# Row maxima of attention scores, taken over two neighbouring PSUM banks by one VectorE instruction

## The chip, the core and the metric

The program runs on one core of a Trainium2 chip. Its engines are TensorE (PE in the profile, its weight loads PEld), VectorE (DVE), ScalarE (ACT), GpSimd (POOL) and SyncE (SP), each with its own instruction queue; they meet only in semaphores and in the shared memories. PSUM, into which TensorE writes, has eight banks of 512 fp32 numbers for each of 128 partitions. The metric is the time on the device in microseconds, the median of several runs.

## The reference

Eight layers run over `x` of 8 sequences x 512 rows x 256 features, each added to its input: four pairs of an attention and a feed-forward part. The change touches the first three, called L0x, L0f and L1x, which share one function. L0x and L1x are plain cross attentions (kind "cross"), L0f is an attention over `x` itself with normalised queries, a temperature and a gate on its output (kind "mixture"). All three have 16 heads of 16 features:

```
q, k, v = heads(norm(x) @ Wq + bq), heads(ctx @ Wk + bk), heads(ctx @ Wv + bv)
attn = softmax(q @ k.T / sqrt(16))        # 512 x 512 for each head
x = x + merge(attn @ v) @ Wo + bo
# L0f: q = (q/|q| + query_embedding) * softplus(temperature); k, v from norm(x);
#      the output is scaled per row by gates from two softmaxes over the heads' output
```

The softmax subtracts each row's maximum before the exponential, and that maximum is what the change is about.

## The kernel before

`softmax_attentions` (L149) treats 24 items, three layers of 8 sequences. An item is one sequence in one layer. For each, q and k are split into bf16 parts, written to a scratch in memory and read back as `qstack` and `kstack`, so that one bf16 matmul with 96 rows gives a score of fp32 quality. Each item has 32 steps, numbered n = 0 to 31, with two units in each. Everything is written out by hand, and each engine runs its own list in the same order of steps:

- `for_maximum` (L753): a matmul with queries as rows, 128 x 512 into one bank of `ps_max`, 12 steps ahead (`LEAD`) of the scores. `maximum` (L482, reduction at L485) is VectorE's maximum over its 512 columns into `maxes`. After 16 units `negated` (L492, L494) writes minus the maxima as two bf16 parts, and TensorE turns them into the shared bank `ps_t` ("negmax", L827). ScalarE casts them into extra rows of `qstack` (L684, 1.86 us).
- `score` (L738, matmul L750): the transposed scores, 104 rows now with the maxima in them, into a bank of `ps_sc`. `exponentials` (L664, L671) is ScalarE's exp of it into `probs`.
- `values` (L774): at n = 1, 5, 9, ... a burst of 16 matmuls of `probs` with v into `ps_out`. ScalarE copies the sum to `heads_raw` (L679).
- Fills of the single bank `ps_t`: `TURNS` is a table of (step, what, which) that says in which step TensorE fills it with projections (k, q, v: L787, L795), transposes (xnT, hT, raw: L782, L833), negated maxima (L827) and output projections (y, L795), for the items one behind to two ahead. Before each fill TensorE waits until the former content was taken, by ScalarE or VectorE. VectorE takes raw by a reciprocal (L511) and a product into `htok` (L513), in its own list behind the maxima of the step before; for a mixture item it takes y into `ffo` (L594) with the scale that the gate arithmetic gives (L561 to L579, steps 20 and 21).

`ps_max` and `ps_sc` have three banks each, `ps_out` and `ps_t` one each, eight together. A matmul into a ring of three waits for the reduction or exponential three units before. The waits are, in `for_maximum` and `score`,

```
if at >= BANKS:
    pe.wait_ge(max_taken, at - BANKS + 1)      # probs_ready in score
```

Of the kernel before, what the change touches and what calls it, by code (L numbers as in the profile page):

```python
# [16 lines left out]
F32 = mybir.dt.float32  # L17
# [4 lines left out]
AX = mybir.AxisListType  # L22

P = 128
SEQS = 8
S = 512
# [78 lines left out]
STEPS = 32  # L105
# [43 lines left out]
def softmax_attentions(nc, T, G, name, kind):  # L149
# [9 lines left out]
    q_part, k_part = part_terms()  # L159
    ROWS = HD * len(q_part)  # L160
    LEAD = 12
    BANKS = 3
    SLOTS = 6
    PER = 4
    x_sb, ident, identb, own_rows = G["x"], G["ident"], G["identb"], G["own"]
    with Phase(nc, name) as ph:
# [21 lines left out]
        qstack = [ph.sb(f"qstack{b}", [ROWS + 8, HEADS, S], BF16) for b in range(2)]  # L188
        kstack = [ph.sb(f"kstack{b}", [ROWS + 8, HEADS, S], BF16) for b in range(2)]
        vpad = [ph.sb(f"vpad{b}", [P, TILES, HEADS * (HD + 1) + 15], F32) for b in range(2)]  # L190
        maxes = ph.sb("maxes", [P, TILES, HEADS], F32)
# [25 lines left out]
        gpart = ph.sb("gpart", [P, TILES], F32)  # L217
        ffo = ph.sb("ffo", [P, 2, D], F32)

        ps_max = ph.ps("ps_max", [P, BANKS, S], F32)  # L220
        ps_sc = ph.ps("ps_sc", [P, BANKS, S], F32)
        ps_out = ph.ps("ps_out", [P, S], F32)
        ps_t = ph.ps("ps_t", [P, S], F32)
# [10 lines left out]
        max_ps, max_taken, neg_step, negmax_ready = (ph.sem("max_ps"), ph.sem("max_taken"), ph.sem("neg_step"),  # L234
                                                     ph.sem("negmax_ready"))
# [21 lines left out]
        def due(q, n):  # L257

            if q.number == -2:
                return [(Item(0), w, c) for m, w, c in FIRST if m == n]  # L260
            near = [q.plus(k) for k in (-1, 0, 1, 2)]
            return [(x, w, c) for x in near if x.there for m, w, c in TURNS[x.kind]
                    if m == n and q.number + shift(w, c) == x.number and (x.later or w != "v")]
# [13 lines left out]
        def weights_here(engine, q):  # L277

            engine.wait_ge(weights_in[LAYERS[q.layer]], n_weights[q.kind])

        def own_key_rows(copy, stack):
            for g in range(4):
                for kt in range(TILES):
                    i = copy(stack[ROWS:ROWS + 8, 4 * g:4 * g + 4, kt * P:(kt + 1) * P], own_rows[ROWS:ROWS + 8])
            return i
# [151 lines left out]
        def _(dve):  # L437
            V = nc.vector
# [33 lines left out]
            def softplus_of_temperature():  # L472
                V.tensor_scalar(tmp1[:], temp[:], -1.0, None, ALU.mult).then_inc(sp_step, 1)
                dve.wait_ge(sp_step, 1)
                V.tensor_tensor(tmp2[:], tmp1[:], temp[:], ALU.min).then_inc(sp_step, 1)
                dve.wait_ge(sp_step, 4)
                V.scalar_tensor_tensor(out=softplus[:], in0=temp[:], scalar=0.0, in1=tmp3[:],
                                       op0=ALU.max, op1=ALU.add).then_inc(sp_step, 1)
                dve.wait_ge(sp_step, 5)
                V.tensor_tensor(qe_soft[:], qe[:], softplus[:], ALU.mult).then_inc(sp_step, 1)  # L480

            def maximum(q, unit):  # L482
                head, t = unit // 4, unit % 4
                dve.wait_ge(max_ps, q.count(64, unit + 1))
                V.tensor_reduce(maxes[:, t, head:head + 1], ps_max[:, q.count(64, unit) % BANKS, :], AX.X,  # L485
                                ALU.max).then_inc(max_taken, 1)

            def negated(q, g):

                own = maxes[:, :, 4 * g:4 * g + 4]  # L490
                dve.wait_ge(max_taken, q.count(64, 16 * g + 16))
                V.tensor_scalar(negmax[:, g % 2, :, :, 0], own, -1.0, None, ALU.mult).then_inc(neg_step, 1)  # L492
                dve.wait_ge(neg_step, q.count(4, g + 1))
                V.scalar_tensor_tensor(out=negmax[:, g % 2, :, :, 1], in0=own, scalar=-1.0,  # L494
                                       in1=negmax[:, g % 2, :, :, 0], op0=ALU.mult,
                                       op1=ALU.subtract).then_inc(negmax_ready, 1)

            def take_v(q, half):

                dve.wait_ge(in_bank["v"], q.count(2, half + 1))  # L500
                V.tensor_tensor(vpad[q.parity][:, 2 * half:2 * half + 2, 0:HEADS * (HD + 1)]
                                .rearrange("p b (h e) -> p b h e", h=HEADS)[:, :, :, 0:HD],
                                ps_t[:].rearrange("p (b h d) -> p b h d", b=2, h=HEADS),
                                weights[q.kind]["bv"][:].rearrange("p (h d) -> p h d", h=HEADS).unsqueeze(1)
                                .broadcast_to([P, 2, HEADS, HD]), ALU.add).then_inc(taken["v"], 1)
# [93 lines left out]
            def steps(q):  # L599
                prev, nxt, ahead = q.plus(-1), q.plus(1), q.plus(2)  # L600
                if nxt.there and nxt.later and nxt.seq == 0:
                    weights_here(dve, nxt)
                for n in range(STEPS):
                    for mine, w, c in due(q, n):
                        if w == "v":
                            take_v(mine, c)
                        if w == "q" and not mine.cross:
                            if c == 0 and mine.seq == 0:
                                weights_here(dve, mine)
                                softplus_of_temperature()  # L610
                            take_q(mine, c)
                        if w == "raw":
                            take_raw(mine, c)
                        if w == "gates":
                            gates_before_exp(mine)
                        if w == "y":
                            take_y(mine, c)
                    m = n + LEAD
                    own = q if m < STEPS else nxt
                    if own.there:  # L620
                        maximum(own, 2 * (m % STEPS))
                        maximum(own, 2 * (m % STEPS) + 1)
                        if m % 8 == 7:
                            negated(own, (m % STEPS) // 8)
                    if prev.there and not prev.cross and n == 20:
                        gates_after_exp(prev)
                    if prev.there and not prev.cross and n == 21:
                        gate_scale(prev)
                    if q.number == -1 and n == 16:

                        own_key_rows(V.tensor_copy, kstack[0]).then_inc(even_own_ready, 1)
                    if not ahead.there:
                        continue
                    if not ahead.cross and n == 12:
                        query_lengths(ahead)
                    if not ahead.later and n == FIRST_K_AT:
                        first_split(taken["k"], kf, kparts, k_step, k_split)
                    if not ahead.later and n == q_at["cross"]:
                        first_split(taken["q"], qf, qparts, q_step, q_split)
                    if ahead.later:  # L640
                        start = NORM_AT[ahead.kind]
                        if n in (start, start + 1):
                            statistics(ahead, (0, 1) if n == start else (2, 3))
                        if n == start + 2:
                            moments(ahead)
                        if n in (start + 4, start + 5):
                            normalised(ahead, (0, 1) if n == start + 4 else (2, 3))
# [5 lines left out]
        def _(act):  # L653
# [10 lines left out]
            def exponentials(q, n):  # L664
# [3 lines left out]
                for j in range(2):  # L668
                    at = q.count(64, 2 * n + j)
                    act.wait_ge(score_ps, at + 1)  # L670
                    nc.scalar.activation(probs[:, step % SLOTS, j], ps_sc[:, at % BANKS, :], ACT.Exp,  # L671
                                         scale=HD ** -0.5).then_inc(probs_ready, 1)
# [63 lines left out]
        def _(pe):  # L736
            weights_here(pe, Item(0))
            def score(q, n, j):  # L738
# [7 lines left out]
                at = q.count(64, 2 * n + j)  # L746
                if at >= BANKS:
                    pe.wait_ge(probs_ready, at - BANKS + 1)
                head = 4 * g + 2 * pair + j
# [3 lines left out]
            def for_maximum(q, unit):  # L753
                head, t = unit // 4, unit % 4
                if unit == 0:
                    pe.wait_ge(stack_in, q.count(192, 192))
                at = q.count(64, unit)
                if at >= BANKS:
                    pe.wait_ge(max_taken, at - BANKS + 1)
                nc.tensor.matmul(ps_max[:, at % BANKS, :], qstack[q.parity][0:ROWS, head, t * P:(t + 1) * P],  # L760
                                 kstack[q.parity][0:ROWS, head, :], start=True, stop=True).then_inc(max_ps, 1)

            def values(q, first, waited):
# [2209 lines left out]
def more_scratch(nc, T):  # L2973
# [4 lines left out]

PHASES = [
    (softmax_attentions, "L0x", ""),  # L2980
    (quantised_ffn, "L1f", ""),
    (feature_attention, "L2x", ""),
# [66 lines left out]
```

## Time and profile before

| what | us |
|---|---|
| median of 3 runs (4497.85 to 4503.6) | 4501.39 |
| the profiled execution | 4504.13 |
| its span | 4502.1 |
| TensorE busy, whole span | 4233.5 (94%) |
| VectorE busy | 2976.9 (66%) |
| ScalarE busy | 2544.5 (57%) |
| VectorE's maxima, L485, 1536 of them | 976.5, 683 ns each |
| ScalarE's exponentials, L671, 1536 of them | 822.7, 607 ns each |

The first 1750 us of the span are the three attentions; the feed-forward of L1 and the later layers follow. Scores start 68.20 us apart from one cross item to the next, and some 72 to 77 us apart in and around the mixture layer. Busy time of TensorE is modelled and overlaps between matmuls: a 512-column bf16 matmul shows 380 ns, but the next may start 0.22 us after it. So the starts of matmuls tell more than their durations. Idle time in square brackets names the instruction that ended it.

### The profile page before, as it was taken

Reading aid. Unit: us, or ns where it says so; the run is one execution under the profiler, and the core shown is the slowest. Engines: PE = TensorE matmul, PEld = TensorE weight load, DVE = VectorE, ACT = ScalarE, POOL = GpSimd, SP = SyncE. Lnnn points to the kernel's source line nnn. Section 1 sums busy time; section 2 is a strip of 40 time slices with the busy share of each in tenths; the row PEclk is TensorE's granted clock in tenths of the full one; section 3 lists DMA queues with packets and bytes.
Section 4 is the critical chain, followed back from the end, with each engine's and each line's share of the span. In section 5 each row is a group of like instructions: output and inputs, shape, how many; then the busy total and the mean of one; then the engine's idle time right before and its main releaser. Section 6 shows DMA issues by size and latency. Waiting matters only on the chain. (4 is left out here: it accounts for less than half of the span.)

```text
span 4502.1 us, 66443 instructions
## 1 busy us (share of the span) xinstructions
PE 4233.5 (94%) x23716; PEld 2403.0 (53%) x23750; DVE 2976.9 (66%) x7431; ACT 2544.5 (57%) x6408; POOL 810.4 (18%) x550
## 2 busy tenths in 40 slices
PE   6999999999999996778989999999999998999999
PEld 2344344444343343567545666666666665555555
DVE  5767777777767776867675666676776766344333
ACT  3767666666667765633555776767676775111111
POOL 2322444443322311523010000000000000000000
PEclk8999999999999998999999999999999999999999
DMA  8456455444456451000100110010101102000000
GB/s 161 73 76 87 65 63 85 54 69 63 74 75 84 69 71 61 1 15 15 75 12 27 31 32 28 30 36 26 33 27 32 32 27 73 5 5 5 10 5 10
DMA packets 182844, 204.97 MB, mean 46 GB/s; under 512 B 44651, under 2 KB 165099, under 8 KB 180854
## 3 DMA queue, kind: packets, MB, share of 16 engines
q1 hardware_dynamic: 180886, 199.15, 24.1%
q8 instruction: 192, 3.15, 0.3%
q10 hardware_dynamic: 1632, 1.57, 0.3%
q14 instruction: 134, 1.10, 0.1%
HBM read 139.90 MB, written 60.78 MB: 45 GB/s over the span
## 5 line engine op out<-in xcount | busy, mean ns | idle before, releaser
L485 DVE TENSOR_REDUCE L0x_maxes<-L0x_ps_max 128x1 f32<-128x512 f32 x1536 | 976.5, 683 | 291.0 <-PE L0x_ps_max L760 289.3
L671 ACT ACTIVATE L0x_probs<-L0x_ps_sc 128x512 f32<-128x512 f32 x1536 | 822.7, 607 | 362.3 <-PE L0x_ps_sc L750 358.3
L760 PE MATMUL L0x_ps_max<-L0x_kstack,L0x_qstack 96*128 96x512 bf16 x1536 | 588.0, 384 | 22.7 <-DVE L0x_maxes L485 21.3
L2756 ACT ACTIVATE L3x_pexp<-L3x_ps,L3x_nmax 128x77 f32<-128x77 f32 (+2 forms) x1536 | 601.4, 433 | 0.0
L750 PE MATMUL L0x_ps_sc<-L0x_qstack,L0x_kstack 104*128 104x512 bf16 x1536 | 557.7, 384 | 11.5 <-ACT L0x_probs L671 11.0
L2638 DVE TENSOR_REDUCE L3x_nmax<-L3x_ps 128x2 f32<-128x154 f32 (+2 forms) x768 | 346.3, 506 | 242.1 <-PE L3x_ps L2869 239.7
L2764 ACT COPY L3x_pT<-L3x_ps 128x512 f32<-128x512 f32 x512 | 275.1, 593 | 225.8 <-PE L3x_ps L2877 225.4
L2256 ACT ACTIVATE L3f_act_g<-L3f_ps_gu 128x512 f32<-128x512 f32 x128 | 76.4, 597 | 542.2 <-PE L3f_ps_gu L2302 542.1
L774 PE MATMUL L0x_ps_out<-L0x_probs,L0x_vpad 128*32 128x512 f32 x3072 | 371.0, 601 | 1.1 <-ACT L0x_probs L671 1.1
L2654 DVE TENSOR_SCALAR L3x_pexp<-L3x_pexp,L3x_rsum 128x77 f32<-128x77 f32 (+2 forms) x1536 | 357.7, 306 | 6.8
L2756 ACT ACTIVATION_READ_ACCUMULATOR L3x_pexp<-L3x_ps,L3x_nmax 128x1 f32 x1536 | 359.4, 235 | 0.0
L2199 DVE TENSOR_TENSOR L3f_h<-L3f_act_g,L3f_ps_gu 128x512 f32<-128x512 f32 x128 | 88.0, 687 | 383.1 <-ACT L3f_act_g L2256 382.9
L760 PEld LDWEIGHTS L0x_ps_max<-L0x_kstack,L0x_qstack 96*128 96x128 bf16 x1536 | 151.0, 98 | 282.5 <-DVE L0x_maxes L485 167.5
L2895 PE MATMUL L3x_ps<-L3x_pT,L3x_v 128*64 128x128 f32 x4096 | 279.9, 279 | 0.7 <-ACT L3x_oT L2772 0.7
L2877 PEld LDWEIGHTS L3x_ps<-ident,L3x_pexp 128*128 128x128 f32 x2048 | 239.1, 141 | 73.4 <-issue 55.5
L2877 PE MATMUL L3x_ps<-ident,L3x_pexp 128*128 128x128 f32 x2048 | 266.1, 273 | 0.9 <-DVE L3x_pexp L2654 0.9
L750 PEld LDWEIGHTS L0x_ps_sc<-L0x_qstack,L0x_kstack 104*128 104x128 bf16 x1536 | 150.6, 98 | 211.7 <-ACT L0x_probs L671 81.1
L2599 POOL TENSOR_TENSOR L3x_v<-L3x_v,L3x_relv 128x256 f32<-128x256 f32 x32 | 23.4, 731 | 1294.7 <-ACT L3x_v L2739 1294.7
L2302 PE MATMUL L3f_ps_gu<-L3f_xnT,L3f_wg 128*128 128x512 f32 x512 | 243.0, 597 | 2.1 <-DMA L3f_wd<-in_L3f_wd 2.1
L2313 PE MATMUL L3f_ps_y<-L3f_wd,L3f_h 128*128 128x256 f32 x1024 | 242.4, 380 | 1.5 <-DVE x_res L2209 1.5
L2895 PEld LDWEIGHTS L3x_ps<-L3x_pT,L3x_v 128*64 128x64 f32 x4096 | 218.3, 136 | 43.4 <-issue 42.5
L2302 PE MATMUL L3f_ps_gu<-L3f_xnT,L3f_wu 128*128 128x512 f32 x512 | 240.6, 592 | 0.0
(377 smaller groups left out, 6841.4 us busy)
## 6 DMA issues: line engine op xcount, KB each, us to landing
L0x_kstack<-parts_scratch SPq DMA_DIRECT2D x141, 256.0 KB, 10.0
L0x_qstack<-parts_scratch SPq DMA_DIRECT2D x141, 256.0 KB, 14.5
parts_scratch<-L0x_kparts SPq DMA_DIRECT2D x24, 768.0 KB, 3.7
parts_scratch<-L0x_qparts SPq DMA_DIRECT2D x24, 768.0 KB, 5.0
rel_scratch<-L3x_rel_e SPq DMA_DIRECT2D x32, 408.0 KB, 2.4
L3x_rel_d<-prob_scratch SPq DMA_DIRECT2D x32, 408.0 KB, 3.1
L0x_kv_in<-in_ctxT SPq DMA_DIRECT2D x16, 512.0 KB, 4.5
L3x_rel_t<-rel_scratch SPq DMA_DIRECT2D x32, 154.0 KB, 2.4
```

Source lines behind the costliest of these rows:

```text
L485: V.tensor_reduce(maxes[:, t, head:head + 1], ps_max[:, q.count(64, unit) % BANKS, :], AX.X, ALU.max).then_inc(max_taken, 1)
L671: nc.scalar.activation(probs[:, step % SLOTS, j], ps_sc[:, at % BANKS, :], ACT.Exp, scale=HD ** -0.5).then_inc(probs_ready, 1)
L750: nc.tensor.matmul(ps_sc[:, at % BANKS, :], kstack[q.parity][:, head, kt * P:(kt + 1) * P], qstack[q.parity][:, head, :], start=True, stop ...
L760: nc.tensor.matmul(ps_max[:, at % BANKS, :], qstack[q.parity][0:ROWS, head, t * P:(t + 1) * P], kstack[q.parity][0:ROWS, head, :], start=T ...
L774: i = nc.tensor.matmul(ps_out[32 * j:32 * j + 32, :], vpad[q.parity][:, kt, (HD + 1) * head:(HD + 1) * head + 32], probs[:, q.count(STEPS, ...
L2302: i = nc.tensor.matmul(ps_gu[:, n % 2, k], w[:, ci, n * P:(n + 1) * P], xnT[:, ci, :], start=(ci == 0), stop=(ci == C - 1))
L2638: i = V.tensor_reduce(nmax[:, n % 4, s], ps[:, bank:bank + 2, a:b], AX.X, ALU.max, negate=True)
L2654: i = V.tensor_scalar(pexp[:, m % 4, e, a:b], pexp[:, m % 4, e, a:b], rsum[:, m % 4, s, e:e + 1], None, ALU.mult)
L2756: i = nc.scalar.activation(pexp[:, n % 4, e, a:b], ps[:, SB + 2 * (n % 2) + e, a:b], ACT.Exp, bias=nmax[:, n % 4, s, e:e + 1], accum_out=s ...
L2764: nc.scalar.copy(pT[:, m % 2, e], ps[:, TB + e]).then_inc(pt_ready, 1)
L2877: i = nc.tensor.transpose(ps[:, TB + e, kt * P:(kt + 1) * P], pexp[:, m % 4, e, kt * P:(kt + 1) * P], ident[:])
L2895: i = nc.tensor.matmul(ps[DIMH * e:DIMH * (e + 1), OB, at:at + P], v[g % 2][:, vt, h * DIMH:(h + 1) * DIMH], pT[:, m % 2, e, kt * P:(kt + ...
```

## The change

The six banks are divided anew: four for maxima, as two neighbouring pairs, and two for scores. TensorE fills both banks of a pair with the two units of a step; VectorE waits for both and takes the maxima of 2 x 512 columns by one instruction. TensorE waits for the release of a pair only ahead of its first matmul. `maximum` becomes `maxima`, `max_taken` counts steps instead of units, and the counts that others wait for follow. Scores keep their code, with `BANKS` 2 in place of 3, so each waits for the exponential two units before. Nothing is computed differently.

```diff
-    BANKS = 3
+    PAIRS_OF_MAXIMA = 2
+    BANKS = 2
...
-        ps_max = ph.ps("ps_max", [P, BANKS, S], F32)
+        ps_max = ph.ps("ps_max", [P, PAIRS_OF_MAXIMA, 2, S], F32)
...
-            def maximum(q, unit):
-                head, t = unit // 4, unit % 4
-                dve.wait_ge(max_ps, q.count(64, unit + 1))
-                V.tensor_reduce(maxes[:, t, head:head + 1], ps_max[:, q.count(64, unit) % BANKS, :], AX.X,
+            def maxima(q, step):
+                head, t = step // 2, 2 * (step % 2)
+                at = q.count(STEPS, step)
+                dve.wait_ge(max_ps, 2 * at + 2)
+                V.tensor_reduce(maxes[:, t:t + 2, head], ps_max[:, at % PAIRS_OF_MAXIMA], AX.X,
                                 ALU.max).then_inc(max_taken, 1)
...
-                dve.wait_ge(max_taken, q.count(64, 16 * g + 16))
+                dve.wait_ge(max_taken, q.count(STEPS, 8 * g + 8))
...
-                        maximum(own, 2 * (m % STEPS))
-                        maximum(own, 2 * (m % STEPS) + 1)
+                        maxima(own, m % STEPS)
...
-                at = q.count(64, unit)
-                if at >= BANKS:
-                    pe.wait_ge(max_taken, at - BANKS + 1)
-                nc.tensor.matmul(ps_max[:, at % BANKS, :], qstack[q.parity][0:ROWS, head, t * P:(t + 1) * P],
+                at = q.count(STEPS, unit // 2)
+                if unit % 2 == 0 and at >= PAIRS_OF_MAXIMA:
+                    pe.wait_ge(max_taken, at - PAIRS_OF_MAXIMA + 1)
+                nc.tensor.matmul(ps_max[:, at % PAIRS_OF_MAXIMA, unit % 2], qstack[q.parity][0:ROWS, head, t * P:(t + 1) * P],
```

No matmul moves in TensorE's list, only its waits do. In the list before, from a burst of value matmuls through the fill with raw heads to the fill with negated maxima, every maximum matmul waits:

```order
L760 MATMUL L0x_ps_max<-L0x_kstack,L0x_qstack 128x512 [waits L0x_max_taken]
L750 MATMUL L0x_ps_sc<-L0x_qstack,L0x_kstack 128x512 [waits L0x_probs_ready]
L760 MATMUL L0x_ps_max<-L0x_kstack,L0x_qstack 128x512 [waits L0x_max_taken]
L833 MATMUL L0x_ps_t<-ident,L0x_heads_raw 128x128 [waits L0x_out_taken,L0x_raw_taken]
L833 MATMUL L0x_ps_t<-ident,L0x_heads_raw 128x128 x3
```

In the changed list at the same place (its lines are one or two further down) every second one does, and the scores' waits look the same but ask for one exponential more:

```order
L761 MATMUL L0x_ps_max<-L0x_kstack,L0x_qstack 128x512 [waits L0x_max_taken]
L751 MATMUL L0x_ps_sc<-L0x_qstack,L0x_kstack 128x512 [waits L0x_probs_ready]
L761 MATMUL L0x_ps_max<-L0x_kstack,L0x_qstack 128x512
L834 MATMUL L0x_ps_t<-ident,L0x_heads_raw 128x128 [waits L0x_out_taken,L0x_raw_taken]
L834 MATMUL L0x_ps_t<-ident,L0x_heads_raw 128x128 x3
```

On VectorE two neighbouring reductions become one in place; what stood behind the second stands behind the wide one.

## Rows read from the trace of the kernel before

**Rows 1.** Windows: us, busy us of PE, PEld, DVE, ACT, POOL, granted clock, DMA, GB/s

```profile
412.76:480.96 68.20, 66.16 (x354) 27.07 (x353) 48.99 (x98) 47.27 (x81) 19.71 (x12) 1.00 0.54 78
```

**Rows 2.** Waits of TensorE's weight loads, 75 to 1750 us: total, times, longest

```profile
PEld L0x_ps_max L760 <- DVE L0x_maxes L485: 158.6, 227, 2.8
...
PEld L0x_ps_sc L750 <- ACT L0x_probs L671: 81.1, 185, 0.9
```

**Rows 3.** VectorE's groups by shape: count, busy us, mean ns, idle before

```profile
L485 DVE TENSOR_REDUCE L0x_maxes<-L0x_ps_max 128x1 f32<-128x512 f32 x1536 | 976.5, 683 | 291.0 <-PE L0x_ps_max L760 289.3
L2638 DVE TENSOR_REDUCE L3x_nmax<-L3x_ps 128x2 f32<-128x838 f32 x256 | 261.1, 1020 | 0.0
...
L2638 DVE TENSOR_REDUCE L3x_nmax<-L3x_ps 128x2 f32<-128x154 f32 x256 | 81.5, 318 | 242.1 <-PE L3x_ps L2869 239.7
```

**Rows 4.** Timeline, steps 2 to 5: start us, us, what; PE, then DVE, then ACT

```profile
417.21 0.60 PE L750 MATMUL L0x_ps_sc<-L0x_qstack,L0x_kstack 104*128 104x512 bf16 x2
...
417.86 0.38 PE L750 MATMUL L0x_ps_sc<-L0x_qstack,L0x_kstack 104*128 104x512 bf16 x1
...
418.34 0.39 PE L750 MATMUL L0x_ps_sc<-L0x_qstack,L0x_kstack 104*128 104x512 bf16 x1
418.56 0.38 PE L760 MATMUL L0x_ps_max<-L0x_kstack,L0x_qstack 96*128 96x512 bf16 x1
...
421.05 0.39 PE L827 MATMUL L0x_ps_t<-identb,L0x_negmax 128*8 128x128 bf16 x4 [0.16 <-DVE L0x_htok L513]
...
417.41 2.54 DVE L485 TENSOR_REDUCE L0x_maxes<-L0x_ps_max 128x1 f32<-128x512 f32 x4 [0.87 <-PE L0x_ps_max L760]
...
420.57 0.42 DVE L513 TENSOR_TENSOR L0x_htok<-L0x_ps_t,L0x_rden 128x256 f32<-128x256 f32 x1
...
417.68 1.09 ACT L671 ACTIVATE L0x_probs<-L0x_ps_sc 128x512 f32<-128x512 f32 x2 [2.24 <-PE L0x_ps_sc L750]
```

**Rows 5.** Timeline, steps 26 to 29 of the item before

```profile
405.54 0.38 PE L760 MATMUL L0x_ps_max<-L0x_kstack,L0x_qstack 96*128 96x512 bf16 x1
...
407.42 0.38 PE L827 MATMUL L0x_ps_t<-identb,L0x_negmax 128*8 128x128 bf16 x4
...
404.30 2.54 DVE L485 TENSOR_REDUCE L0x_maxes<-L0x_ps_max 128x1 f32<-128x512 f32 x4 [2.94 <-PE L0x_ps_max L760]
...
404.67 1.08 ACT L671 ACTIVATE L0x_probs<-L0x_ps_sc 128x512 f32<-128x512 f32 x2
```

**Rows 6.** Timeline, steps 14 to 16 (374 us), 21 to 25 (393 to 400 us)

```profile
374.43 1.34 DVE L485 TENSOR_REDUCE L0x_maxes<-L0x_ps_max 128x1 f32<-128x512 f32 x2 [1.35 <-PE L0x_ps_max L760]
...
376.45 0.48 PE L795 MATMUL L0x_ps_t<-L0x_wo_cross,L0x_hT 128*128 128x256 f32 x1
...
399.67 0.39 PE L750 MATMUL L0x_ps_sc<-L0x_qstack,L0x_kstack 104*128 104x512 bf16 x1
...
393.63 3.17 ACT L671 ACTIVATE L0x_probs<-L0x_ps_sc 128x512 f32<-128x512 f32 x6
...
399.03 1.56 ACT L671 ACTIVATE L0x_probs<-L0x_ps_sc 128x512 f32<-128x512 f32 x3
```

**Rows 7.** Timeline, steps 30 to 1, across the start of an item at 412.76

```profile
414.21 0.39 PE L760 MATMUL L0x_ps_max<-L0x_kstack,L0x_qstack 96*128 96x512 bf16 x1
...
414.80 0.39 PE L760 MATMUL L0x_ps_max<-L0x_kstack,L0x_qstack 96*128 96x512 bf16 x1
...
412.87 2.47 DVE L485 TENSOR_REDUCE L0x_maxes<-L0x_ps_max 128x1 f32<-128x512 f32 x4
```

**Rows 8.** Mixture item, step 23: timeline of PE and DVE, then the window behind it

```profile
983.56 0.39 PE L760 MATMUL L0x_ps_max<-L0x_kstack,L0x_qstack 96*128 96x512 bf16 x1 [2.55 <-DVE L0x_maxes L485]
983.79 0.38 PE L795 MATMUL L0x_ps_t<-L0x_wo_mixture,L0x_hT 128*128 128x256 f32 x1
...
982.03 0.88 DVE L594 SCALAR_TENSOR_TENSOR L0x_ffo<-L0x_ps_t,L0x_gscale,L0x_bo_mixture 128x256 f32<-128x256 f32 x2
...
984.00:988.00 4.00, 4.00 (x13) 2.35 (x12) 2.71 (x6) 0.80 (x2) 3.92 (x3) 0.59 0.26 88
```

## The prediction

> **What bounds the kernel now.** The page's chain of waits covers only the last stage, the gated experts, so I read the stage that the change touches, the first 1750 us, from views of its own. First the windows: one sequence of a cross layer takes 68.20 us, and TensorE is busy for 66.16 of them, VectorE for 48.99 (72%), ScalarE for 47.27 (69%) [rows 1]. TensorE is the bound, and it works through one fixed order. What counts is therefore how long that order stands still, not how busy another engine is. Next the waits: weight loads of TensorE wait 158.6 us for the release of a bank of maxima [rows 2]. Most of that lies under matmuls still running, so it is a ceiling. The true loss is read from the starts of matmuls, which follow one another by 0.22 us when nothing holds them (418.34, 418.56) [rows 4]. Read in this way, a steady cross sequence loses about 1.3 us to maxima: 0.50 at steps 0 and 1, where the matmul of 414.21 is one of three held up [rows 7], and the rest at steps 8 and 13. In a mixture sequence one such wait alone is 2.55 us [rows 8].
>
> **The change, part by part.** Three things happen. (1) 1536 reductions of 512 become 768 of 1024. (2) The reduction starts when the second of its two matmuls is in, and frees both banks at its end. (3) Scores have two banks, so score i waits for exponential i-2, not i-3. TensorE's order of instructions stays.
>
> *Width.* Back to back, four reductions take 2.48 to 2.54 us, so a further one costs 0.60 [rows 4, 5], two 1.20. A wide one is not in this stage, but the same instruction form elsewhere reads PSUM: 154 elements in 318 ns, 838 in 1020, which is 1.03 ns an element and gives 1.21 us for 1024 [rows 3]. Bounds: 1.13 (1.21 less the overlap of 0.08 seen between neighbours) and 1.37 (two times the 683 ns of a narrow one). I take 1.21 to the end, 1.13 in a row. That saves 0.07 x 768 = 54 us of VectorE's work, none of it on the path by itself. The Trainium skill, "Perfetto Trace Analysis", section "Optimizing Scalar/DVE Operations", gives about 125 ns of fixed cost for an instruction on PSUM and says that grouping pays when the engine is saturated; by its figure the saving would be an estimated 96 us of work. The row of 72% says that the engine is not saturated. The same section says that where an unsaturated engine leaves bubbles on others, breaking instructions up may help, which is against this change.
>
> *What it does to the path.* I walked one steady cross sequence of 32 steps in bundles of four, each from one burst of value matmuls to the next, since the burst (1.86 us) lets both helpers catch up. Rules, from rows: a matmul's result starts ScalarE or VectorE 0.42 to 0.47 us after the matmul starts (417.21 to 417.68), exponentials follow by 0.49 and last 0.60, and the freed matmul starts 0.06 after their end (418.28 to 418.34) [rows 4].
>
> Steps 2 to 5, +0.74. Scores of step 3 now wait for the exponentials of step 2, ending 418.28 and 418.77: they start at 418.34 and 418.83 instead of 417.86 and 418.34. The second maximum matmul of step 3 goes from 418.56 to 419.06; the wide reduction starts at 419.48 and ends at 420.69, where four narrow ones ended at 419.95 [rows 4]. Behind it on VectorE are negation, reciprocal and the product into htok, and TensorE's fill of the shared bank ps_t at 421.05 waits for exactly that product. It comes 0.74 later.
>
> Steps 26 to 29, +0.82. The same: exponentials of step 26 from 404.67 to 405.75 put the second maximum matmul of step 27 from 405.54 to 406.03, its reduction ends at 407.66, not 406.84, and the fill with the negated maxima goes from 407.42 to 408.24 [rows 5].
>
> Steps 14 to 17 and 22 to 25, +0.53 each. Two reductions, 1.34 us from 374.43, end at 375.77; the wide one can start when the second narrow one did, since both wait for the second matmul (375.77 - 0.68 = 375.09), and ends at 376.30. The products behind it and the fill at 376.45 that waits for them come 0.53 later [rows 6]. One row stands for both places.
>
> Third score bank, bare, +0.84 more. At step 21 the second score waits 0.19 longer and at step 22 0.16 more, for exponentials that resume at 393.63 after a cast: +0.35. At step 25 the exponentials from 399.03 free the score of 399.67 only at 400.17: +0.49 [rows 6].
>
> Steps 30 to 1, +0.54. The product behind the wide reduction of step 30 is 0.76 late. The reduction of step 31 starts at 413.63 instead of 412.87 and ends at 414.84, so the matmul of 414.21 starts at 414.90; the last before the burst goes from 414.80 to 415.34 [rows 7]. The waits of 0.50 at steps 0 and 1, which the change is aimed at, are swallowed by this.
>
> Steps 6 to 9, +0.09 (the 0.49 wait for a maximum goes, scores lose 0.59); steps 10 to 13, -0.05 (0.17 gained, 0.12 lost behind the negation).
>
> Sum: 0.74 + 0.82 + 1.06 + 0.84 + 0.54 + 0.09 - 0.05 = 4.04 us on 68.20.
>
> *Mixture sequences*, walked in the same way, have the same bundles at steps 26 to 1 (+0.82, +0.54), +1.02 in steps 14 to 17 (0.53 behind the product, 0.49 for the score bank), and +0.20 and +0.23 in steps 2 to 5 and 10 to 13: +2.8. Against it, VectorE's long gate arithmetic makes TensorE wait 2.55 us for a maximum of step 23, to 983.56 [rows 8]. With four banks that matmul is free, but the next instruction, the second output fill, needs ffo, ready at 982.91 and 0.34 later by the wide reductions ahead of it: the fill goes from 983.79 to 983.3, 0.5 saved, and 1.9 us of standstill remain, that is 0.7 less. From 984 to 988 the granted clock is 0.59 [rows 8], which is mostly its lower level of 1.2 GHz, behind that standstill. In these 4 us TensorE starts 13 matmuls where 18 would fit at 0.22, so if the shorter standstill keeps the clock, some 1.2 us come back as well. I take that: 2.8 - 0.5 - 1.2, about +1.2 a sequence with rounding up; if not, +2.3.
>
> *Total.* Of 24 sequences some 12 are steady cross (12 x 4.04 = 48), 5 are full mixture with the gate wait (5 x 1.2 = 6), 7 lie between (7 x 3.2 = 22, taken between the two kinds): +76 us. The rest of the program is untouched. The profiled execution took 4504.1 for a span of 4502.1; the sum is made against it, and the median of the runs shown is 4501.4, so 4501.4 + 76 = 4577.
>
> **Rivals.** *Faster.* The 1.3 us of a cross sequence and 3.7 of a mixture one that maxima cost today disappear and nothing comes in their place: 12 x 1.3 + 7 x 1.8 + 5 x 3.7 = 47, or 4454. For it: VectorE is 0.07 faster a pair and leads by four banks. It decides if the fills of ps_t do not stand right behind the chain maxima, negation, product; the rows show them 0.06 behind (420.99 to 421.05). [...] *Only the VectorE half holds.* If scores lose nothing, the four fills still come 0.25, 0.53, 0.53 and 0.33 late, and 1.2 is saved: +0.4 x 24, or 4510. Against it: the third bank is used whenever a score starts before exponential i-2 has ended, as at 417.86 against 418.28. *The clock.* If the added stops bring the lower clock once in most sequences, as after 984, 1.2 us x 20 comes on top: 4601. Against it: each added stop is under 1 us, and the sequence at 412.76 to 480.96, with several such, has clock 1.00 [rows 1]. *Width.* At 1.37 us a reduction, four fills are 0.16 later: +0.6 x 24, 4592, inside my range.
>
> **How the numbers follow.** About 0.2% (9 us) can be told from no change. Forecast 0.72, faster rival 0.07, VectorE half alone 0.11 (it straddles the border: half of it counts as same, some as slower), clock 0.10. Range 4530 to 4608: below, half of what I let add up is absorbed by other waits; above, the clock or the width. Faster 0.07, same 0.06, slower 0.87.
>
> **What would show it.** In the profile after: a wide reduction of 1.21 us; a steady cross sequence of about 72.2 us; waits of TensorE for the exponentials (now 81.1 us ahead of weight loads [rows 2]) clearly up, those for maxima down, those for htok and negmax up by 0.5 to 0.8 a place; the clock at the gate stop of five sequences near 1. Wrong would be a period of 68 or less, or fills that no longer stand behind htok.

## The result and the profile after

The changed kernel takes 4589.19 us, the median of four runs (4588.57 to 4590.2); the kernel before took 4502.5 beside it. The ratio is 1.019, 95% interval 1.0177 to 1.0203: slower by 87 us. The profiled execution has a span of 4588.2 us against 4502.1.

The attentions carry all of it. Their last score starts at 1835.0 us in the trace after and at 1746.6 before, 88.4 later; what follows is 2.4 shorter. The 24 sequences are numbered 0 to 23 from here on: 0 to 7 are of L0x, 8 to 15 of the mixture layer, 16 to 23 of L1x. First a steady cross sequence, number 5, the same one as in [rows 1]; the columns are those of that group:

```profile
430.30:502.35 72.05, 66.87 (x353) 26.07 (x354) 47.31 (x66) 48.02 (x81) 19.68 (x12) 1.00 0.51 74
```

It takes 72.05 us, where it took 68.20. VectorE has less to do (47.31 for 48.99), TensorE keeps its full clock, and the time went up by 3.85. The waits of TensorE over the three layers, 75 to 1840 us (total, times, longest; first weight loads, then matmuls):

```profile
PEld L0x_ps_sc L751 <- ACT L0x_probs L672: 263.3, 611, 1.1
...
PEld L0x_ps_max L761 <- DVE L0x_maxes L487: 94.9, 137, 0.8
```

```profile
PE L0x_ps_sc L751 <- ACT L0x_probs L672: 39.8, 113, 0.6
PE L0x_ps_t L828 <- DVE L0x_negmax L496: 20.9, 40, 2.3
PE L0x_ps_t L828 <- DVE L0x_htok L515: 20.9, 23, 0.9
PE L0x_ps_t L788 <- DVE L0x_htok L515: 9.1, 16, 0.6
PE L0x_ps_t L796 <- DVE L0x_htok L515: 8.1, 16, 0.6
```

Against [rows 2], waits for maxima fell from 158.6 to 94.9 and waits for exponentials rose from 81.1 to 263.3. New names stand among the waits of the matmuls: fills of `ps_t` wait for `htok` and `negmax`. The wide reduction itself, in VectorE's groups by shape (75 to 1840 us, so 758 of the 768), takes 1221 ns, for two of 683 in [rows 3]:

```profile
L487 DVE TENSOR_REDUCE L0x_maxes<-L0x_ps_max 128x2 f32<-128x1024 f32 x758 | 919.3, 1221 | 417.4 <-PE L0x_ps_max L761 415.6
```

Steps 3 to 5 of the same sequence, which answer to [rows 4]:

```profile
435.80 0.39 PE L751 MATMUL L0x_ps_sc<-L0x_qstack,L0x_kstack 104*128 104x512 bf16 x1 [0.32 <-ACT L0x_probs L672]
...
436.29 0.39 PE L751 MATMUL L0x_ps_sc<-L0x_qstack,L0x_kstack 104*128 104x512 bf16 x1
...
436.52 0.38 PE L761 MATMUL L0x_ps_max<-L0x_kstack,L0x_qstack 96*128 96x512 bf16 x1
...
436.93 1.23 DVE L487 TENSOR_REDUCE L0x_maxes<-L0x_ps_max 128x2 f32<-128x1024 f32 x1 [0.18 <-PE L0x_ps_max L761]
...
438.19 0.18 DVE L494 TENSOR_SCALAR L0x_negmax<-L0x_maxes 128x16 bf16<-128x16 f32 x1
...
438.78 0.42 DVE L515 TENSOR_TENSOR L0x_htok<-L0x_ps_t,L0x_rden 128x256 f32<-128x256 f32 x1
...
439.26 0.39 PE L828 MATMUL L0x_ps_t<-identb,L0x_negmax 128*8 128x128 bf16 x4 [0.89 <-DVE L0x_htok L515]
```

This is the chain of the prediction, link by link: the scores 0.49 apart behind exponentials, the last maximum matmul at 436.52, the wide reduction 0.41 behind it, then negation, reciprocal and product, and the fill 0.06 after the product's end. The fill's idle time in brackets is 0.89 where [rows 4] has 0.16.

### The profile page after: what moved, and what is told of

It is laid out like the page before. It is cut to its first block and busy times, and to the rows that moved or that the text cites. A ratio compares the mean times of both kernels' runs of the same rounds, so it can differ in the third digit from the quotient of the medians.

```text
span 4588.2 us, 65675 instructions
## 1 busy us (share of the span) xinstructions
PE 4264.7 (93%) x23716; PEld 2376.5 (52%) x23750; DVE 2940.4 (64%) x6663; ACT 2561.3 (56%) x6408; POOL 808.7 (18%) x550
## 5 line engine op out<-in xcount | busy, mean ns | idle before, releaser
L487 DVE TENSOR_REDUCE L0x_maxes<-L0x_ps_max 128x2 f32<-128x1024 f32 x768 | 931.0, 1221 | 429.3 <-PE L0x_ps_max L761 427.5
L672 ACT ACTIVATE L0x_probs<-L0x_ps_sc 128x512 f32<-128x512 f32 x1536 | 841.6, 603 | 386.1 <-PE L0x_ps_sc L751 374.0
L751 PEld LDWEIGHTS L0x_ps_sc<-L0x_qstack,L0x_kstack 104*128 104x128 bf16 x1536 | 149.0, 97 | 373.6 <-ACT L0x_probs L672 263.3
L2878 PE MATMUL L3x_ps<-ident,L3x_pexp 128*128 128x128 f32 x2048 | 266.1, 273 | 0.9 <-DVE L3x_pexp L2655 0.9
```

The lines of the kernel that those rows point to most:

```text
L487: V.tensor_reduce(maxes[:, t:t + 2, head], ps_max[:, at % PAIRS_OF_MAXIMA], AX.X, ALU.max).then_inc(max_taken, 1)
L751: nc.tensor.matmul(ps_sc[:, at % BANKS, :], kstack[q.parity][:, head, kt * P:(kt + 1) * P], qstack[q.parity][:, head, :], start=True, stop ...
L2878: i = nc.tensor.transpose(ps[:, TB + e, kt * P:(kt + 1) * P], pexp[:, m % 4, e, kt * P:(kt + 1) * P], ident[:])
```

## The experiments

The table shows eight stretches of a steady cross sequence in four kernels, with the time that TensorE's starts lose in each: the distance of a start to the next, less what the same instruction takes when nothing holds it (0.22 us for a maximum or score). The two kernels in the middle are experiments and follow below. Stretches run from one burst of value matmuls to the next.

| steps | before | 4 + 2 banks, narrow | and started late | after | after - before | predicted |
|---|---|---|---|---|---|---|
| 2 to 5 | 1.09 | 1.41 | 1.89 | 1.83 | +0.74 | +0.74 |
| 6 to 9 | 0.66 | 0.75 | 0.76 | 0.76 | +0.09 | +0.09 |
| 10 to 13 | 1.38 | 1.19 | 1.46 | 1.33 | -0.05 | -0.05 |
| 14 to 17 | 0.66 | 0.63 | 1.25 | 1.18 | +0.52 | +0.53 |
| 18 to 21 | 0.49 | 0.67 | 0.67 | 0.68 | +0.19 | +0.19 |
| 22 to 25 | 0.48 | 1.11 | 1.71 | 1.65 | +1.17 | +1.18 |
| 26 to 29 | 1.09 | 1.49 | 1.98 | 1.91 | +0.82 | +0.82 |
| 30 to 1 | 0.51 | 0.55 | 0.56 | 0.82 | +0.32 | +0.54 |
| period | 68.2 | 69.7 | 72.2 | 72.05 | +3.85 | +4.04 |

The eight differences add up to 3.80; the other 0.05 us of the period is not in stops that this table counts.

**The banks alone.** Two kernels keep 1536 narrow reductions, each started by its own matmul. The first has three banks for maxima and two for scores, the second four and two. Their edit, with `MAX_BANKS` 3 or 4:

```diff
-    BANKS = 3
+    MAX_BANKS = 3
+    BANKS = 2
...
-                if at >= BANKS:
-                    pe.wait_ge(max_taken, at - BANKS + 1)
-                nc.tensor.matmul(ps_max[:, at % BANKS, :], qstack[q.parity][0:ROWS, head, t * P:(t + 1) * P],
+                if at >= MAX_BANKS:
+                    pe.wait_ge(max_taken, at - MAX_BANKS + 1)
+                nc.tensor.matmul(ps_max[:, at % MAX_BANKS, :], qstack[q.parity][0:ROWS, head, t * P:(t + 1) * P],
```

> The kernel before with two score banks in place of three; maxima stay narrow in three banks, one bank unused. Theory (two causes add up: the missing third score bank, and the later end of the wide reduction ahead of the ps_t fills): the missing bank alone costs about 1.9 us of a steady cross sequence (68.2 to 70.1), some 42 us in all, near 4545. Rival A (the score bank costs everything, the width nothing): about 4589, as the changed kernel. Rival B (the wide reduction costs everything): 4502.

> Four banks for maxima and two for scores as in the changed kernel, but one narrow reduction for each bank, so only the width differs from the changed kernel. Theory: waits for maxima fall below those of three banks, the score waits stay, a steady cross sequence takes about 69.9 us, total near 4535; the width is then the other 55 us. Rival A: 4589, as with the wide reduction. Rival B: 4502 or less.

Measured: 4543.18, ratio 1.0086 (1.0071 to 1.0101), and 4531.66, ratio 1.006 (1.0045 to 1.0075); a steady cross period is 69.9 and 69.7. Taking the third bank from the scores costs 38 us. In the first kernel it lies idle; giving it to the maxima, as the second does, buys back 12, mostly outside the steady sequences. Both times come within 4 us of what was expected. Not all of the 38 is waits for a bank: sequence 8 takes 5.3 us of it, and there a negation that otherwise lasts 0.18 us takes 2.15 beside a GpSimd instruction, of which the last experiment tells. The fourth bank does not pay for the third one that the scores lose.

**The late start alone.** The kernel before, with one number changed: the first reduction of a step waits for the second matmul too. Then the same on top of four banks for maxima and two for scores, which makes it the changed kernel in everything except the width.

```diff
-                dve.wait_ge(max_ps, q.count(64, unit + 1))
+                dve.wait_ge(max_ps, q.count(64, 2 * (unit // 2) + 2))
```

> The kernel before, three and three banks, with one wait stretched: the first of the two narrow reductions of a step also waits for the step's second matmul. Nothing else changes. Theory: the late start is what costs in the wide reduction, since the fills of ps_t stand behind it; the end of the second reduction comes 0.6 us later after each burst, about +2.4 us in a steady cross sequence plus some 0.5 at three banks, total near 4565. Rival A (only the score bank costs): within 5 us of 4502.

> Four banks for maxima, two for scores, narrow reductions, but the first reduction of a step waits for the step's second matmul, as the wide one must. Against the run with four narrow banks (4531.7) only that wait is added; against the changed kernel only the width differs, with the wide reduction 0.06 us shorter than the two narrow ones. Theory: the late start is the whole cost of the wide reduction, so this takes what the changed kernel takes or up to 0.06 us x 4 a sequence more, 4589 to 4597. Rival (something else in the wide instruction costs, such as its reading of two banks against TensorE's writes): near 4532 to 4545.

Measured: 4592.97, ratio 1.0195 (1.018 to 1.021), and 4579.92, ratio 1.0172 (1.0155 to 1.0189). Both miss, the first by 28 us, the second by 9 below its range. With three banks the late start was dearer than expected, as dear as the whole change: the period is 72.2, and the negations held in sequences 6 and 7 take 2.13 us. The ring of three is short for pairs: weight loads wait 266.1 us for maxima (158.6 before, [rows 2]):

```profile
PEld L0x_ps_max L760 <- DVE L0x_maxes L485: 266.1, 491, 3.1
```

With four banks the period is 72.19, within 0.14 of the changed kernel's. The steps 3 to 5 of this kernel, in sequence 5 again:

```profile
437.08 2.70 DVE L486 TENSOR_REDUCE L0x_maxes<-L0x_ps_max 128x1 f32<-128x512 f32 x4 [0.97 <-PE L0x_ps_max L761]
...
440.41 0.42 DVE L514 TENSOR_TENSOR L0x_htok<-L0x_ps_t,L0x_rden 128x256 f32<-128x256 f32 x1
...
440.89 0.33 PE L828 MATMUL L0x_ps_t<-identb,L0x_negmax 128*8 128x128 bf16 x3 [0.96 <-DVE L0x_htok L514]
```

In a steady sequence the change is then two prices and a rebate: 1.54 for the banks (68.19 to 69.73), 2.46 for the late start (69.73 to 72.19), and 0.14 back for the width. In the table the late start stands at five places, each with a fill of `ps_t` behind VectorE: 0.48, 0.27, 0.62, 0.60 and 0.49, together 2.46. The rebate is a net figure. Most stretches gain, 0.39 together, and steps 30 to 1 lose 0.26. There a maximum at step 1 waits 0.31 for the wide reduction, which frees its two banks only at its end; with narrow reductions, started just as late, no maximum waits there.

The whole program does not follow the steady sequences. The changed kernel takes 9.3 us more than the one with four banks and late narrow reductions, though each steady sequence takes 0.14 less. The difference lies mostly in sequences 6 to 8: 75.6, 72.9 and 73.0 us there, 80.3, 78.2 and 76.6 in the changed kernel. It is no price of the width as such, but of where VectorE's small instructions meet GpSimd's, which the last experiment takes up: once they are kept apart in sequences 6 to 8, the changed kernel takes 4575.71, 4.2 less than this one. The 48 us from 4531.66 to 4579.92 are not the late start alone either: sequence 8 gets 2.3 us shorter by it, 75.3 to 73.0, since the negation that was held there is no longer.

**The opposite split.** Two banks for maxima, four for scores, narrow reductions (`MAX_BANKS = 2`, `BANKS = 4` in the first diff).

> The kernel before with two banks for maxima, four for scores, narrow reductions: the opposite division. Theory (each ring pays with its own turnround: matmul to release takes 0.42 + 0.60 + 0.06 = 1.1 us at ScalarE, 0.42 + 0.68 + 0.06 = 1.2 at VectorE, so a ring of two stops TensorE wherever four score and maximum matmuls stand within 0.88 us, whichever ring it is): the maxima ring of two costs at least what the score ring of two cost (38 us), rather more since a reduction is longer: 4545 to 4560, a cross period of 70 to 70.7. Rival (only scores are short of banks, maxima have slack, and a fourth score bank takes away the waits of 0.5 us at steps 21 to 29): 4490 to 4500, faster than before.

Measured: 4567.7 (4558.56 to 4568.96), ratio 1.0139 (1.0122 to 1.0156). The cross period is 70.7, at the upper end of what was expected; the time lies 8 us above the range, and the full mixture sequences take 78.5 us (75.3 to 76.6 before). Its two windows, one cross and one mixture sequence, and its wait for maxima:

```profile
430.67:501.39 70.72, 67.85 (x354) 27.00 (x353) 49.10 (x98) 47.61 (x81) 19.68 (x12) 1.00 0.52 75
955.74:1034.25 78.51, 73.15 (x386) 32.93 (x385) 58.45 (x122) 47.91 (x82) 34.15 (x15) 0.96 0.45 61
```

```profile
PEld L0x_ps_max L761 <- DVE L0x_maxes L486: 338.4, 673, 3.5
```

A bank more for either ring is paid for by the other. Three and three is the best of the four splits that were run.

**Another step for the raw heads.** If the late chain maxima, negation, product is what counts, fills that do not wait for `htok` at once should give it room. The fill with raw heads goes two steps later or one earlier, so that the fill behind it is a step further away. The table is edited alike in the changed kernel and in the one before; the fence shows pieces of its lines.

```diff
-    "cross": [(4, "raw", 3), (5, "negmax", 1), (9,
+    "cross": [(5, "negmax", 1), (6, "raw", 3), (9,
...
-(14, "xnT", 0), (15, "raw", 0), (16, "y", 0)
+(14, "raw", 0), (15, "xnT", 0), (16, "y", 0)
...
-(23, "raw", 1), (24, "q", 0), (26, "q", 1), (29, "negmax", 0), (31, "raw", 2)
+(22, "raw", 1), (24, "q", 0), (26, "q", 1), (29, "negmax", 0), (30, "raw", 2)
```

(In the mixture table 4, 15, 25 and 31 become 6, 17, 26 and 30.)

> The changed kernel with the raw fills of ps_t moved so that each comes right behind a burst of value matmuls or has no fill in the step after it (cross: steps 4, 15, 23, 31 to 6, 14, 22, 30, with xnT 0 from 14 to 15; mixture: 4, 15, 25, 31 to 6, 17, 26, 30). VectorE then has taken raw before the next fill asks. Theory: the waits of fills for htok (0.79, 0.89 and 0.53 of 1.06 us in a cross sequence) go, about -2 us a sequence, near 4545. Rival (the fills wait for something else that ends at the same time, or the product moves and the wait with it): within 10 us of 4589.

> The kernel before with the raw fills moved as in the run on the changed kernel. There the waits for htok went, but scores, no longer kept apart by the raw fills, gave 1.3 of 2.3 us back with two banks. Theory (three banks of scores do what the fills did): here the waits for htok (0.32, 0.34, 0.36 us a sequence) and for the heads (0.64) go and little comes back, about -1.2 us a sequence, near 4478. Rival (the give-back is in ScalarE's pace whatever the banks): 4495 to 4505.

Measured: 4582.56, ratio 1.0171 (1.0154 to 1.0188), and 4518.81, ratio 1.0031 (1.0018 to 1.0044). Both miss their forecasts of 4545 and 4478, the second on the other side of no change. The chain did get its room: on the changed kernel the lost time at steps 5, 16 and 24 goes from 1.06, 0.80 and 0.89 to 0.53, 0.08 and 0. But the period falls only from 72.05 to 71.08. Steps 4 and 5 of sequence 5 show where the rest went:

```profile
433.38 0.39 PE L751 MATMUL L0x_ps_sc<-L0x_qstack,L0x_kstack 104*128 104x512 bf16 x1 [0.37 <-ACT L0x_probs L672]
...
434.85 0.22 PE L828 MATMUL L0x_ps_t<-identb,L0x_negmax 128*8 128x128 bf16 x1 [0.37 <-DVE L0x_negmax L496]
```

The raw fill at step 4 had also been the work that TensorE did while ScalarE caught up. Without it the scores of step 4 wait 0.54, where they had waited for nothing, and those of steps 23 and 31 0.48 each. In the kernel before the same happens with three banks (the raw fill's own wait of 0.64 at step 4 goes, a score's wait of 0.54 comes, and a maximum of step 8 waits 0.31 longer), its period goes from 68.2 to 68.3, and all but one of the mixture sequences become longer. What I had overlooked is that ScalarE falls behind TensorE at the same places as VectorE, and that a fill is cover for both.

**GpSimd's hold on VectorE.** In sequences 6 to 8, where the mixture layer begins, the change cost 6.7, 6.9 and 5.3 us instead of the 3.2 that I had put down. The first of them ends so in the trace after (GpSimd, VectorE, then TensorE, and the window behind it):

```profile
571.61 2.12 POOL L381 TENSOR_TENSOR L0x_qparts<-L0x_qf,L0x_qparts 128x1024 bf16<-128x1024 f32 x1
571.66 2.11 DVE L494 TENSOR_SCALAR L0x_negmax<-L0x_maxes 128x16 bf16<-128x16 f32 x1
...
573.80 0.18 DVE L496 SCALAR_TENSOR_TENSOR L0x_negmax<-L0x_maxes,L0x_negmax 128x16 bf16<-128x16 f32 x1
...
574.12 0.58 PE L828 MATMUL L0x_ps_t<-identb,L0x_negmax 128*8 128x128 bf16 x4 [2.29 <-DVE L0x_negmax L496]
...
575.04 0.63 PE L761 MATMUL L0x_ps_max<-L0x_kstack,L0x_qstack 96*128 96x512 bf16 x1
```

```profile
574.10:578.10 4.00, 3.98 (x16) 1.15 (x20) 2.23 (x2) 2.94 (x3) 0.00 (x0) 0.50 0.56 197
```

A negation of 16 numbers a partition, 0.18 us elsewhere, takes 2.11, starts 0.05 after an instruction of GpSimd and ends with it. TensorE waits 2.29 us for the negation and then works at a granted clock of 0.50, the lower of its two levels (1.2 GHz). Before, the negation fell into the second half of the GpSimd instruction ahead of that one, and lasted 0.90 us in sequence 6, 0.91 in 7 and 1.26 in 8. The rows of sequence 7:

```profile
618.15 1.90 POOL L378 TENSOR_TENSOR L0x_qparts<-L0x_qf,one 128x1024 bf16<-128x1024 f32 x1
619.18 0.91 DVE L492 TENSOR_SCALAR L0x_negmax<-L0x_maxes 128x16 bf16<-128x16 f32 x1
```

In the kernel with four banks and late narrow reductions no negation of these three sequences lasts over 0.23 us: in sequence 6 its two halves start at 573.54 and 573.81, the second GpSimd instruction at 573.82.

To test this, GpSimd's second half of that split of q is made to wait until the next item's first negation is over, in the changed kernel. In the kernel before a second such wait goes with it, which holds the second half of the split of k back until the gate arithmetic is done; and last, both waits in the changed kernel. In the edit the wait for `gate_step` is the one on k, the wait for `negmax_ready` behind it the one on q.

```diff
+                    if ahead.later and after_k == 1 and not ahead.cross and q.there and q.plus(-1).there and not q.plus(-1).cross:
+                        pool.wait_ge(gate_step, q.plus(-1).own(15, 15))
+                    if ahead.later and after_q == 2 and not ahead.cross and q.plus(1).there:
+                        pool.wait_ge(negmax_ready, q.plus(1).count(4, 1))
                     if ahead.later and after_k in (0, 1):
```

> The changed kernel, in which GpSimd holds back the second half of its split of a mixture item's q parts until the next item's first negation is done. Theory: the negation of 2.11 us in three sequences, which ends with GpSimd's operation, is VectorE held by GpSimd; without it these three sequences (80.3, 78.2, 76.6 us) lose about 2 us of standstill and part of their lower clock each, total 4580 to 4583. Rival (the long negation has another cause): the three stay as long, total 4589.

> The kernel before, with the same hold on the q parts and another: the second half of the split of k parts in mixture items waits for the end of the gate arithmetic. Theory: the two gate operations of 1.75 and 1.97 us, which end with GpSimd's operations in the kernel before, fall to about 0.2 us, the standstill of 2.55 us at step 23 in five sequences goes with the low clock behind it, and the three negations of 0.9 to 1.3 us go: about -3.5 us x 5 and -0.8 x 3, near 4484. Rival (GpSimd's later splits delay the stacks, or the operations are long for another reason): 4500 or more.

> The changed kernel with both waits of GpSimd: its second half of the q split of a mixture item waits for the next item's first negation, its second half of the k split for the gate arithmetic of the item before. Theory (a fixed price per sequence of the wide maximum and the two score banks, on top of which GpSimd holds VectorE in the mixture layer): with the first wait alone the changed kernel took 4575.7, its full mixture items 76.1 to 77.4; without the held gate operations these fall by some 2 us each in 5 items, to about 74.5, and the time to about 4565. Against the old kernel with both waits (4485.0) that leaves +80, or 24 x 3.3. Rival (the gate stop of the changed kernel is set by the wide reductions ahead of the gate arithmetic, not by GpSimd): nothing, 4574 to 4577.

Measured: the changed kernel with the first wait 4575.71, ratio 1.016 (1.0145 to 1.0175); with both 4565.74, ratio 1.0141 (1.0126 to 1.0156); the kernel before with both **4484.98, ratio 0.996 (0.9945 to 0.9975)**, faster than either kernel. The first is 4 us below its range, the other two within 1 us of what was expected. The negation and what starts it, with the first wait in place:

```profile
570.64 0.18 DVE L496 TENSOR_SCALAR L0x_negmax<-L0x_maxes 128x16 bf16<-128x16 f32 x1
...
571.11 1.89 POOL L379 TENSOR_TENSOR L0x_qparts<-L0x_qf,one 128x1024 bf16<-128x1024 f32 x1 [2.57 <-DVE L0x_negmax L498]
```

Sequences 6 to 8 fall from 80.3, 78.2 and 76.6 to 75.6, 73.3 and 73.0: 13.1 us, for a median that is 13.5 lower. In the gate arithmetic the second wait does the same. First the changed kernel, then the kernel before with both waits:

```profile
1023.65 1.75 DVE L576 SCALAR_TENSOR_TENSOR L0x_gpart<-L0x_gshare,L0x_gsw 128x4 f32<-128x4 f32 x1
...
1025.46 2.12 POOL L381 TENSOR_TENSOR L0x_kparts<-L0x_kf,L0x_kparts 128x1024 bf16<-128x1024 f32 x1
1025.63 1.97 DVE L579 SCALAR_TENSOR_TENSOR L0x_gtop<-L0x_gsw,L0x_gshare 128x4 f32<-128x4 f32 x1
...
1028.76 1.99 PE L796 MATMUL L0x_ps_t<-L0x_wo_mixture,L0x_hT 128*128 128x256 f32 x8 [1.27 <-DVE L0x_ffo L596]
```

```profile
965.88 0.16 DVE L578 SCALAR_TENSOR_TENSOR L0x_gpart<-L0x_gshare,L0x_gsw 128x4 f32<-128x4 f32 x1
...
966.27 0.16 DVE L581 SCALAR_TENSOR_TENSOR L0x_gtop<-L0x_gsw,L0x_gshare 128x4 f32<-128x4 f32 x1
...
966.72 1.89 POOL L378 TENSOR_TENSOR L0x_kparts<-L0x_kf,one 128x1024 bf16<-128x1024 f32 x1 [1.09 <-DVE L0x_gscale L583]
```

Two instructions on four numbers a partition took 3.72 us together and take 0.32. A full mixture sequence in four kernels: before, after, before with both waits, after with both waits:

```profile
924.91:1000.21 75.30, 70.27 (x386) 32.27 (x385) 58.14 (x122) 47.57 (x82) 34.12 (x15) 0.98 0.45 64
```

```profile
969.04:1045.63 76.59, 70.02 (x385) 30.03 (x386) 57.03 (x90) 48.02 (x82) 34.11 (x15) 1.00 0.47 62
```

```profile
913.07:985.38 72.31, 68.82 (x385) 31.43 (x384) 54.73 (x123) 47.47 (x82) 34.10 (x15) 1.00 0.50 66
```

```profile
950.38:1025.44 75.06, 69.76 (x385) 30.11 (x384) 53.33 (x91) 48.04 (x83) 34.11 (x15) 1.00 0.48 64
```

With nothing held the change costs 2.75 us a mixture sequence, and 2.70 to 2.85 in each of the sequences 6 to 8. The two long instructions of the gate arithmetic, which I had taken as given, were GpSimd's doing.

## Why the prediction came out as it did

Forecast 4577, measured 4589.2. The sum of 76 us stands against 86 in the span. The mechanism that was walked is the one that the runs show; the sizes of two terms were off, and a third mechanism, GpSimd's hold on VectorE, was missing.

- **The width**: 1.21 assumed, 1.22 measured, 1.13 in a row. VectorE's busy time fell by 1.68 us in a steady sequence of 32 pairs, 0.05 a pair, where the sum had 0.07 and the estimate from the page 0.125. The width saved 0.14 us of path a sequence, not nothing but next to it.
- **The steady cross sequence**: +4.04 assumed, +3.85 measured. Seven of the eight stretches agree to 0.01. The term that was off is steps 30 to 1, 0.54 for 0.32: there the late reduction does swallow the old waits for maxima, but less is left at steps 0 and 1 (two scores held 0.24 and 0.20, one maximum 0.31) than I carried over. The twelve sequences that I had counted as steady gave 43.7 for 48 (the ten in the middle 3.86 each, the first 0.7, the last but one 4.4).
- **The full mixture sequences**: +1.2 each assumed, 7.3 for the five measured (6 assumed). The walk of +2.8 agrees with the kernels with both waits (2.77 on the mean of the five), in part by luck. From burst to burst these two differ in sequence 12 by 0.21, 0.24 and 1.02 where 0.20, 0.23 and 1.02 were walked, by 0.75 at steps 26 to 29 (0.82) and again by 0.31 at steps 30 to 1 (0.54), and by 0.22 at steps 18 to 21, where nothing was put down. The stop behind the gate shrank further than foreseen: TensorE is idle for 1.27 us ahead of the fill, where it had stopped for 2.55 [rows 8] and I had left 1.9. The clock was kept in two of the five, as in the window above with 1.00 (before 0.98), and these rose by 1.0 and 1.3. In two others the window still shows 0.98, and they rose by 2.1 and 2.2, close to the 2.3 I had given for that case; the fifth rose by 0.7, from one that had 0.96 before. So the same stop was followed by the lower clock in three of the five, and the traces do not tell why not in the other two.
- **The sequences between**: this is the term that was mis-sized, 22 assumed and 36 measured. Seven times 3.2 was an interpolation between the two kinds, not a walk. Sequences 6 to 8 took 18.9 of it. The walk's own part there is 8.3 (the kernels with both waits); the rest is the held negation and the lower clock behind it, which no reading of a steady sequence could have given. The rows were there, though: a negation of 0.91 us among those of 0.18. Sequences 14 to 16 took 3.7, 4.3 and 2.9. The first two contain a spell at the lower clock that they had not before: their windows go from 1.00 to 0.98, and inside the first a fill of four fp32 matmuls with keys takes 3.39 us, 1.95 before, with the granted clock at 0.54:

```profile
1164.09 3.39 PE L788 MATMUL L0x_ps_t<-L0x_kv_in,L0x_wk_cross 128*128 128x512 f32 x4
```

```profile
1164.00:1167.40 3.40, 3.40 (x6) 1.34 (x6) 1.23 (x1) 1.30 (x3) 0.00 (x0) 0.54 0.00 0
```

```profile
1115.85 1.95 PE L787 MATMUL L0x_ps_t<-L0x_kv_in,L0x_wk_cross 128*128 128x512 f32 x4
```

(The last line is of the kernel before.) That is 1.4 us, and without it the sequence is at 2.3. No stop of over 1 us stands right ahead of this spell, and it is there with both waits of GpSimd too, so its cause stays open. The last sequence with its end took 6.2 and was not taken apart.
- **Not in the sum**: the first score is 1.4 later, and what follows the attentions 2.4 shorter. Together that is -1.0, left open.
- **The rivals.** Faster: most of the waits for maxima did go. By the starts of matmuls a steady sequence lost 1.16 us to them before (0.50 at steps 0 and 1, 0.49 at step 8, 0.17 at step 13; the prediction rounded up to 1.3) and loses 0.31 after. Waits for exponentials and the fills of `ps_t` took their place. VectorE half alone: the score bank by itself costs 38 us, and 27 with a fourth bank for maxima, so it falls. The clock: it did cost, in sequences 6 to 8, 14 and 15, which had 1.00 before, while the steady ones stay at 1.00; it is in the mixture layer and its neighbours, not behind the small stops that the change adds everywhere. Width: 1.22, not 1.37.

## What to carry to other kernels

One instruction over two banks starts with the later of its two producers and frees both banks at its end. On an engine that has room this buys little (0.14 us a sequence) and costs the chains that end behind it 0.27 to 0.62 us each (2.5 us a sequence), while the banks it needs come from someone else's ring. Ask first which consumers stand right behind the instruction and what work covers the wait there, and look for tiny VectorE instructions that last as long as a GpSimd instruction beside them: two waits for GpSimd brought 19 us here, more than any division of the banks.

## What the runs showed of the hardware

Small VectorE instructions were held while GpSimd ran a tensor_tensor of 128x1024 with both inputs in SBUF, above all the negations (128x16 fp32 to bf16), and two products of the gate arithmetic with two SBUF inputs of 128x4. They take 0.16 to 0.18 us elsewhere, took up to 2.15 here, and ended 0.02 to 0.04 us after GpSimd's instruction. The Trainium skill, "SBUF — State Buffer", section "🔬 SBUF: two separate sides", calls the port pair that the two engines share an exclusive lock, held by whoever comes first for its whole instruction; the trace agrees (571.61 and 571.66 above). It names VectorE instructions with two SBUF inputs or in a two-port mode. The negation held at 571.66 has one tensor input, so of the two only a two-port mode could fit it, and no run here tells the mode.

Not every small instruction is held. A sum over 128x60 fp32 in SBUF, with one input and fp32 output, ran its 0.20 us inside a GpSimd instruction in the changed kernel, in each of the five full mixture sequences:

```profile
1019.28 1.89 POOL L374 TENSOR_TENSOR L0x_kparts<-L0x_kf,one 128x1024 bf16<-128x1024 f32 x1 [5.19 <-DVE L0x_negmax L496]
1020.82 0.20 DVE L563 TENSOR_REDUCE L0x_gsum<-L0x_gexp 128x4 f32<-128x60 f32 x1
```

The maxima, which read PSUM, were not held either: in the changed kernel none of the 768 took over 1.23 us, and 307 of them overlap a tensor_tensor of GpSimd.

And a wait of 2.29 us of TensorE was followed by the lower clock level, one of 1.27 us behind the gate in three of five cases, while steady sequences with a dozen stops of up to 0.9 us kept 1.00.
